# Two cross-attention stages of a fused Perceiver block on one core, unrolled and put into another order of a step

## The reference

```python
q, k, v = split_heads(x @ wq + bq), split_heads(ctx @ wk + bk), split_heads(ctx @ wv + bv)
attn = softmax(q @ k.T / sqrt(16) + neg)     # neg from the mask, xa0 only
attn = attn * group_prob                     # xa0 only
x = x + (attn @ v).reshape(B, S, 256) @ wo + bo
```

## Time and profile before

| | us |
|---|---|
| median of 3 runs | 1098.29 (1097.12 to 1099.25) |
| profiled execution, its own time | 1096.61 |
| its span, first to last instruction | 1094.7 |
| TensorE busy | 839.2 (77% of the span) |
| VectorE busy | 548.9 (50%) |
| ScalarE busy | 446.4 (41%) |
| GpSimd busy | 397.8 (36%) |
| xa0 on TensorE, from its first query projection to sa's first matmul | 187.5 |
| xa1 on TensorE, to ssm's first matmul | 195.9 |

### The profile page before, as it was taken

How to read it: one execution, slowest core, us unless ns; L and a number is a source line. 1 busy time by engine, 2 the same in 40 slices (tenths; PEclk the granted TensorE clock), 3 DMA queues, 4 the chain that set the end, 5 groups by cost and what they waited for, 6 DMA issues and landing times.

```text
span 1094.7 us, 21754 instructions
## 1 busy us (share of the span) xinstructions
PE 839.2 (77%) x6944; PEld 590.6 (54%) x6944; DVE 548.9 (50%) x1397; ACT 446.4 (41%) x1527; POOL 397.8 (36%) x577
## 2 busy tenths in 40 slices
PE   1899989689879658888987462677453999999990
PEld 0666666478754226666665341566341466666660
DVE  2477777568744343655655577576432222222222
ACT  1566666346614224656564102466400233333320
POOL 3356465535458754243344534222425000000005
PEclk9999999899969888999998765777655999999995
DMA  8121112633241634343233200211167034443004
GB/s 320 42 56 46 49 48 65 237 104 109 88 154 46 196 105 136 104 137 106 96 106 123 97 0 12 86 40 40 49 229 279 16 132 153 145 140 131 16 21 120
DMA packets 63723, 114.37 MB, mean 104 GB/s; under 512 B 6304, under 2 KB 20384, under 8 KB 62880
## 3 DMA queue, kind: packets, MB, share of 16 engines
q1 hardware_dynamic: 55488, 103.15, 28.0%
q10 hardware_dynamic: 6624, 6.03, 1.7%
q0 software_dynamic: 1536, 4.20, 1.3%
HBM read 79.02 MB, written 34.34 MB: 104 GB/s over the span
## 4 chain that ended last, share of the span: by engine, by line
PE 45%; ACT 15%; DVE 15%; POOL 10%; issue 9%; DMA 4%; SPq 1%; DVEq 0%; ACTq 0%; POOLq 0%
ACT probs L1116 6%; PE ps L967 4%; PE ps L969 4%; PE ps L968 4%; PE ps L524 3%; ACT probs L1075 3%; PE ps L567 3%; PE ps L583 2%; DMA ctx_t<-in_ctx 2%; DVE stat L1478 2%; PE ps L990 2%; PE ps L992 2%; PE ps L991 2%; ACT probs L1066 2%; PE ps L979 2%
## 5 line engine op out<-in xcount | busy, mean ns | idle before, releaser
L1266 POOL TENSOR_TENSOR var<-mv,half 128x1 f32<-128x1 f32 x56 | 11.0, 196 | 288.5 <-DVE mv L1479 201.2
L1298 POOL TENSOR_TENSOR piece_out<-piece_in,piece_out 128x512 f16<-128x512 f32 x96 | 112.7, 1173 | 7.7
L1966 DVE TENSOR_TENSOR probs<-ps,ctx_t 128x512 f32<-128x512 f32 x46 | 29.6, 686 | 155.0 <-PE ps L969 155.0
L567 PE MATMUL ps<-pack_const,probs 128*128 128x128 f32 x512 | 78.7, 291 | 28.8 <-DVE vbuf L1520 11.3
L1461 POOL DMA_INDIRECT pt<-y_rows,neg x16 | 15.4, 962 | 234.2 <-DMA y_rows<-vbuf 229.7
L1323 POOL TENSOR_TENSOR probs<-probs,gp 128x512 f32<-128x512 f32 x64 | 81.3, 1303 | 51.1 <-ACT probs L1066 51.1
L567 PEld LDWEIGHTS ps<-pack_const,probs 128*128 128x128 f32 x512 | 58.7, 146 | 53.2 <-DVE vbuf L1520 13.1
L1297 POOL CAST piece_out<-piece_in 128x512 f16<-128x512 f32 x96 | 62.2, 648 | 41.9 <-DMA piece_in<-in_w 40.7
L967 PE MATMUL ps<-arena,qbuf 128*128 x184 | 71.0, 386 | 0.0
L968 PE MATMUL ps<-arena,qbuf 128*128 x184 | 70.8, 385 | 0.0
L969 PE MATMUL ps<-arena,qbuf 128*128 x184 | 70.8, 385 | 0.0
(11 more groups left out here) (246 smaller groups left out, 2000.3 us busy)
## 6 DMA issues: line engine op xcount, KB each, us to landing
piece_in<-in_w SPq DMA_DIRECT2D x96, 256.0 KB, 2.8
w_parts<-piece_out SPq DMA_DIRECT2D x96, 256.0 KB, 2.0
arena<-w_parts SPq DMA_DIRECT2D x8, 3072.0 KB, 12.6
ctx_t<-in_ctx SPq DMA_DIRECT2D x32, 256.0 KB, 2.7
x_rows<-piece_out SPq DMA_DIRECT2D x1, 2944.0 KB, 16.7
qbuf<-x_rows ACTq DMA_DIRECT2D x23, 128.0 KB, 2.5
y_rows<-vbuf ACTq DMA_DIRECT2D x23, 128.0 KB, 1.7
arena<-in_xa SPq DMA_DIRECT2D x2, 1282.0 KB, 7.1
```

The source lines that it names most:

```text
L567: last = pe.transpose(AB[:, o:o + P], pr[:, 2 * c + n, kt * P:(kt + 1) * P], ident)
L1298: pool.tensor_tensor(both[:, PIECE:], src, both[:, 0:PIECE], ALU.subtract).then_inc(piece_split, 1)
```

## The change

All five engines run `step(k)` for k = 0 to 20 (`CROSS_STEPS` = `SEQS` + 5), each step with code of its own. Scores of a sequence are issued in one go, chunks 2 and 3 of a sequence move one step later, the mixed values to the end of a step, the steps that close a tile one step or more later. The context and the summed values have three buffers each; the third ones lie in unused columns of `qbuf`. The turned reciprocals move from AB[0:256] to M[256:512]. The diff, cut to its core and with the indentation reduced:

```diff
+spare = qbuf[:, :].bitcast(F32)
+contexts = [ctx_t[:, 0:DC * KEYS], ctx_t[:, DC * KEYS:2 * DC * KEYS], spare[:, 1024:1536]]
+values_of = [v32[:, 0:512], v32[:, 512:1024], spare[:, 1536:2048]]
+return 16 * (b // 3 + 1) + (16 * len(range(b % 3, SEQS, 3)) if st == "xa1" else 0)
+CROSS_STEPS = SEQS + 5
-    hold(sp, G[st]["v_projected"], b - 1)
+    hold(sp, G[st]["v_projected"], b - 2)
+    sp.dma_start(contexts[b % 3], src).then_inc(ctx_loaded[b % 3], 16)
...
-    def load_step(k, s, h):
-        if live(k, 0, SEQS):
-            load_context("xa0", k, s)
-        if live(k, 1, SEQS):
-            load_mask(k - 1, 1 - s)
-    skewed(sp, SEQS, 1, load_step)
+    for b in range(2, SEQS):
+        if b + 1 < SEQS:
+            load_context("xa0", b + 1)
+        load_mask(b, b % 2)
...
-    if k + 2 < SEQS:
-        load_context("xa1", k + 2, k % 2)
+    if 1 <= k < SEQS - 2:
+        load_context("xa1", k + 2)
...
-            hold(pe, g["r_copied"], b - 2)
+            hold(pe, g["pt_act"], 2 * b - 5)
-            hold(pe, g["pt_dve"], 2 * b - 2)
+            hold(pe, g["pt_dve"], 2 * b - 3)
+        hold(pe, g["xt"], h - 3)
+        hold(pe, g["resid"], h - 2)
...
             hold(pe, g["weighted"], 4 * b + c + 1)
             if c == 0:
-                hold(pe, g["k_copied"], at_most(b + 3, SEQS))
-                if isinstance(b, int) and b + 2 >= SEQS:
-                    hold(pe, g["r_copied"], b)
+                if b == 0:
+                    hold(pe, g["k_copied"], 3)
+                hold(pe, g["pt_act"], 2 * b)
             elif c == 1:
-                hold(pe, g["v_summed"], at_most(b + 2, SEQS))
-                if isinstance(b, int) and b + 1 >= SEQS:
-                    hold(pe, g["pt_dve"], 2 * b)
+                if b == 0:
+                    hold(pe, g["v_summed"], 2)
+                hold(pe, g["pt_dve"], 2 * b)
+            elif c == 2:
+                hold(pe, g["k_copied"], at_most(b + 4, SEQS))
+                hold(pe, g["pt_act"], 2 * b + 1)
             else:
-                hold(pe, g["pt_act" if c == 2 else "pt_dve"], 2 * b + 1)
+                hold(pe, g["v_summed"], at_most(b + 3, SEQS))
+                hold(pe, g["pt_dve"], 2 * b + 1)
...
         hold(pe, g["r_spread"], b + 1)
-        hold(pe, g["pt_act"], 2 * b + 2)
+        hold(pe, g["o_normed"], b)
         for f in range(2):
-            last = pe.transpose(AB[:, f * P:(f + 1) * P], spread[:, f * P:(f + 1) * P], ident)
+            last = pe.transpose(M[:, 256 + f * P:256 + (f + 1) * P], spread[:, f * P:(f + 1) * P], ident)
+        v = values_of[b % 3].rearrange("p (k n) -> p k n", k=2)
+        hold(pe, g["r_copied"], b + 1)
...
-    def step(k, s, h):
         if live(k, 0, SEQS):
-            if s == 0:
-                project_queries(h)
-            project_keys(k, s, h)
+            if k % 2 == 0:
+                project_queries(k // 2)
+            project_keys(k)
+        if live(k, 1, SEQS):
+            project_values(k - 1)
         if live(k, 3, SEQS):
-            mix_values(k - 3, 1 - s)
+            turn_reciprocals(k - 3)
+            turn_probs(k - 3, (k - 3) % 2, (2,))
+        if k % 2 == 1 and live(k, 5, SEQS):
+            join_heads((k - 5) // 2)
+        if k % 2 == 0 and live(k, 6, SEQS):
+            hold(pe, g["q_taken"], at_most(k // 2 + 1, TILES))
+            turn_rows(g, k // 2 - 3)
+        if live(k, 3, SEQS):
+            turn_probs(k - 3, (k - 3) % 2, (3,))
         if live(k, 1, SEQS):
-            project_values(k - 1, 1 - s)
-        for hf in range(2):
-            if live(k, 2, SEQS):
-                turn_probs(k - 2, s, (2 * hf, 2 * hf + 1))
-            if hf == 1 and live(k, 2, SEQS):
-                turn_reciprocals(k - 2)
-            if hf == 1 and live(k, 3, SEQS) and s == 0:
-                join_heads(h - 2)
-            if hf == 0 and live(k, 4, SEQS) and s == 1:
-                hold(pe, g["xt"], h - 2)
-                turn_rows(g, h - 2)
-            if live(k, 1, SEQS):
-                score(k - 1, 1 - s, h - 1 if s == 0 else h, hf)
-    skewed(pe, SEQS, 4, step)
+            for hf in range(2):
+                score(k - 1, (k - 1) % 2, (k - 1) // 2, hf)
+        if live(k, 2, SEQS):
+            turn_probs(k - 2, k % 2, (0, 1))
+        if live(k, 3, SEQS):
+            mix_values(k - 3, (k - 3) % 2)
+    for k in range(CROSS_STEPS):
+        step(k)
...
-        act.activation(turned_r[:, s * D:(s + 1) * D], AB[:, 0:D], ACT.Copy).then_inc(g["r_copied"].sem, 1)
+        act.activation(turned_r[:, s * D:(s + 1) * D], M[:, 256:512], ACT.Copy).then_inc(g["r_copied"].sem, 1)
+    def step(k):
+        pairs = range(PAIRS)
+        if live(k, 2, SEQS):
+            if st == "xa0":
+                exps(k - 2, k % 2, pairs)
+            else:
+                plain_exps(k - 2, k % 2, pairs[:4])
         if live(k, 0, SEQS):
-            copy_keys(k, s)
+            copy_keys(k, k % 2)
         if live(k, 2, SEQS) and st == "xa1":
-            plain_exps(k - 2, s)
-        for hf in range(2):
-            if live(k, 2, SEQS):
-                copy_probs(k - 2, s, 2 * hf)
-            if hf == 0 and live(k, 4, SEQS) and s == 1:
-                copy_turned(g, h - 2)
+            plain_exps(k - 2, k % 2, pairs[4:])
+        if live(k, 3, SEQS):
+            copy_reciprocals(k - 3, (k - 3) % 2)
+            copy_probs(k - 3, (k - 3) % 2, 2)
+        if k % 2 == 0 and live(k, 6, SEQS):
+            copy_turned(g, k // 2 - 3)
         if live(k, 2, SEQS):
-            copy_reciprocals(k - 2, s)
-        if live(k, 0, SEQS) and s == 0:
-            copy_queries(h)
-        if live(k, 1, SEQS) and st == "xa0":
-            exps(k - 1, 1 - s)
-    skewed(act, SEQS, 4, step)
+            copy_probs(k - 2, k % 2, 0)
+        if k % 2 == 0 and live(k, 0, SEQS):
+            copy_queries(k // 2)
+    for k in range(CROSS_STEPS):
+        step(k)
...
+    def step(k):
+        h = k // 2
+        if k % 2 == 0 and live(k, 0, SEQS):
             hold(pool, prev["normed"], h + 1)
             add_bias(g, h, w["bo"], prev["resid"] if st == "xa1" else prev["normed"])
+        if k % 2 == 0 and live(k, 6, SEQS):
+            root_of_variance(g, h - 3)
+        if live(k, 2, SEQS) and st == "xa0":
+            weigh(k - 2, k % 2)
         if live(k, 1, SEQS) and st == "xa0":
-            negate_mask(k - 1, 1 - s, h - 1 if s == 0 else h)
-        if live(k, 3, SEQS) and s == 0:
-            root_of_variance(g, h - 2)
-        if live(k, 1, SEQS) and st == "xa0":
-            weigh(k - 1, 1 - s)
-        if st == "xa1" and live(k, 3, SEQS) and s == 0:
-            hold(pool, g["normed"], h - 1)
+            negate_mask(k - 1, (k - 1) % 2, (k - 1) // 2)
+        if st == "xa1" and k % 2 == 0 and live(k, 6, SEQS):
+            hold(pool, g["normed"], h - 2)
             settle()
-            pool.tensor_copy(tile(xn_all, h - 2), xn[:, :]).then_inc(g["kept"].sem, 1)
-        if st == "xa1":
+            pool.tensor_copy(tile(xn_all, h - 3), xn[:, :]).then_inc(g["kept"].sem, 1)
+        if st == "xa1" and k < SEQS + 4:
             for j in range(2):
                 split_piece(j, k + XA1_PIECES // 2)
         chain.restart()
-    skewed(pool, SEQS, 4, step)
+    for k in range(CROSS_STEPS):
+        step(k)
...
-        hold(dve, g["pv_done"], b - 1)
+        hold(dve, g["pv_done"], b - 2)
-        on = scratch[:, 512:768]
-        chain.link(dve.tensor_tensor(on, M[:, 0:256], turned_r[:, s * D:(s + 1) * D], ALU.mult))
+        one, two_ = M[:, 256:384], scratch[:, 512:640]
+        chain.mark(dve.tensor_tensor(by_f(two_), sums[:, :, 1, :], shares[:, :, 1, :], ALU.mult))
+        chain.link(dve.tensor_tensor(by_f(one), sums[:, :, 0, :], shares[:, :, 0, :], ALU.mult))
-    def step(k, s, h):
-        closes = live(k, 3, SEQS) and s == 0
+    def step(k):
+        h = k // 2
+        if live(k, 2, SEQS):
+            (mask_scores if st == "xa0" else row_maxima)(k - 2, k % 2)
+        if live(k, 3, SEQS):
+            copy_probs(k - 3, (k - 3) % 2, 1)
+            spread_reciprocals(k - 3, (k - 3) % 2)
+        if live(k, 4, SEQS):
+            normalise_outputs(k - 4, k % 2, h - 2)
+        if k % 2 == 0 and live(k, 6, SEQS):
+            if st == "xa1":
+                hold(dve, g["kept"], h - 3)
+            hold(dve, g["turned"], h - 3)
+            normalise(g, h - 3, xn[:, :])
+        if k % 2 == 0 and live(k, 0, SEQS):
             take_queries(h)
+        if live(k, 1, SEQS):
+            sum_values(k - 1)
         if live(k, 3, SEQS):
-            normalise_outputs(k - 3, 1 - s, h - 2 if s == 0 else h - 1)
-        if live(k, 1, SEQS):
-            sum_values(k - 1, 1 - s)
-        if live(k, 2, SEQS):
-            copy_probs(k - 2, s, 1)
-            spread_reciprocals(k - 2, s)
-            copy_probs(k - 2, s, 3)
-        if closes:
-            add_output(g, h - 2, C[:, 256:512])
-            tile_stats(g, h - 2)
-        if live(k, 1, SEQS):
```

(58 more changed lines are left out.)

39 lines of the change are left out of this document (17 added, 22 removed).

## The result

The changed kernel takes 1059.82 us in the median (1056.85 to 1060.41, 4 runs) beside 1097.70 of the kernel before on the same chip: ratio 0.9646, interval 0.9619 to 0.9673. Its profiled execution took 1059.76 us with a span of 1057.9, so the span fell by 36.8 us. The forecast of 1065 and its range hold.

The account below looks back on a forecast made before the run. TensorE was taken as the bound, the rest as waits. Gains of 8.7 + 3.2 - 2 (xa0) and 20.8 + 4.1 - 2 (xa1), together 33 us, took 1096.61 to 1063.6; 1.7 more gave 1065, range 1050 to 1080 (own range 1054 to 1071).

Parts of the forecast that it names:

- (1): Both stages: issuing a sequence's scores in one burst instead of two halves saves 0.27 us a step, 0.5 a pair.
- (2): Both stages' regular parts: a pair of steps without any wait takes 18.8 us in xa0 and 19.0 in xa1.
- (3): xa0's six pairs: new waits of 1.1 and 0.35 us make a pair 20.2 us, gaining 1.45 each, 8.7 in all.
- (4): xa1's six pairs: no wait left, a pair takes 19.0 us, gaining 3.5 each, 20.8 in all.
- (5): Stage ends: first parts 23.9 and 26.5 us, tails 29.9 and 30.0; net gain taken as 3.2 and 4.1.
- the clock's share: Tails of both stages: 2 us a stage taken off the gain for matmuls at half speed.
- (6): Tails of both stages: gaps between matmul bursts send the clock back to 1.2 GHz, costing 2 us a stage.
- ACT keeping xa0 where it is: Rival, chance 0.18: small latencies between engines keep xa0's pairs at 21.7 us, only xa1 gains; 1074 us.
- POOL or transfers binding xa1: Rival, chance 0.10: POOL's pieces, stretched by transfer contention, make xa1's pairs 20.5 to 21.5 us; 12 us lost, 1077.
- Waits changing places: Rival, chance 0.03: TensorE's reciprocals wait for DVE's normalising and take back the gain; 1096 to 1100 us.
- Slower through code: Rival, chance 0.05: some 20 more steps of code, each fetch exposed for 2.7 us, add 54 us; 1119 us.

## Why the prediction held, step by step

The sum was right to 3.8 us of 33, out of terms that were off by more and in opposite directions, so that it came this close is in part luck.

**(1) The burst**: 0.27 us a step forecast. Between the same marks score groups cover 17.1 us of twelve steps before and 13.75 after in either stage, 0.28. Right in size. That it also shortens the step is shown for xa1; splitting the scores again made xa0's pairs 0.7 us longer.

**(2) A pair without waits** was mis-sized: 18.8 and 19.0 forecast, 18.0 measured in xa1 (107.9 / 6). TensorE's busy time fell by 12.0 us there (119.1 to 107.1), where I took off 6. The score groups give 3.4. The other groups' own sums fell by some 4: values from 24.0 to 22.8, since they took 2.00 us behind the mixing and take 1.90 behind the keys; joining from 6.8 to 6.2 and reciprocals from 5.5 to 4.6, of which the run with the loop written out has 6.2 and 4.9 already. The remaining 4 to 5 us are overlap of groups, which I had priced at 0.07 us a wait.

**(3) xa0**: 20.2 a pair forecast, 115.7 / 6 = 19.3 measured. The mechanism is as forecast, in place and in which steps: chunk 2 for the key copy in odd steps, 0.84 for 1.1, and chunk 3 for the value sum in even ones, 0.20 for 0.35. Idle time is 6.3 / 6 = 1.05 a pair for 1.45, and the rest is the gap-free pair, 18.2 for 18.8. That this wait is the price of xa0 was too simple: taken away, the same time stood at DVE, and at POOL after that. One term of DVE had the wrong sign. I added 0.15 us a step for a third operation of the normalising. Its sum of the two heads' parts before, in xa0's pairs:

```profile
L1574 DVE TENSOR_TENSOR ot<-scratch 128x128 f32<-128x128 f32 x12 | 13.8, 1153 | 0.4
```

With the operation ahead of it (421 ns) the normalising took 1.57 us a step; the three of now take 278, 283 and 292 ns, 0.85 us. That the change thus makes this step 0.7 us shorter on DVE, the forecast did not have. The spreading of the reciprocals, priced at no change, rose from 425 to 805 ns.

**(4) xa1**: no wait left, as forecast; the pair 18.0 for 19.0, by step (2). The contexts wait no more, but my step named the third buffer among the causes, and both runs on it say that it is none.

**(5) The first parts** failed: 23.9 and 26.5 forecast, 28.1 in both measured. (The net of xa0's ends has a slip besides: 6.5 - 2.9 is 3.6, not 3.4.) TensorE in xa0's, and DVE in step 3:

```profile
29.53 3.62 PE L531 MATMUL ps<-ctx_t,arena 128*128 128x256 f32 x8
...
49.95 2.94 PE L543 MATMUL ps<-arena,qbuf 128*128 128x256 f32 x8 [1.96 <-DVE pt L1552]
```

```profile
46.44 0.42 DVE L1577 CUSTOM_DVE_ANT_0 probs<-ps,neg 128x256 f32<-128x256 f32 x1 [2.05 <-POOL neg L1337]
```

The values of sequence 2 wait 1.96 us for DVE's copy of chunk 1, which in step 3 stands behind eight masks, and these wait 2.05 us for the negated mask, which stands behind POOL's first weighing; I had followed that copy in the regular steps only. The negation's place is what counts. In the run that negates first the copy still stands behind the masks, and the values wait 0.38 us; with that run's other edit alone, the key copy's, they wait 2.39. The row of the run that negates first:

```profile
48.35 1.99 PE L543 MATMUL ps<-arena,qbuf 128*128 128x256 f32 x8 [0.38 <-DVE pt L1552]
```

Of the 4.2 us missed, 2.3 belong to one execution. The run with the pieces last has the same code up to there and the same wait (1.95 us), and its first part took 25.8 us: its first keys took 2.48 us for 3.62, and its granted clock was 1.00 for 0.94. In xa1's first part the scores of sequence 1 wait for the exponentials of sequence 0, a wait that my step does not name, and behind it the granted clock was 0.69 (419.5 to 425.0):

```profile
419.57 2.09 PE L595 MATMUL ps<-kbuf,qbuf 32*128 32x256 f32 x16 [2.54 <-ACT probs L1091]
```

The tails: 33.0 and 32.9 us for 31.9 and 32.0 with the clock's share. POOL's last root stands behind four pieces, as forecast, and one piece waits 2.96 us for its load besides.

**(6) The clock**: 0.90 and 0.93 in the tails, higher than the 0.87 and 0.79 of before, though TensorE was busy a smaller share of them (60 and 53% for 64 and 64%), so this term can't be read off as a loss. It filled in for waits of the tails' chains, such as these of xa0:

```profile
175.87 2.58 PE L543 MATMUL ps<-arena,ctx_t 128*128 128x256 f32 x8 [2.35 <-DVE pt L1552]
...
187.86 0.66 PE L604 MATMUL ps<-pack_const,scratch 128*128 128x128 f32 x2 [3.90 <-DVE ot L1602]
```

In all, the pairs gave 40.6 us for 29.5, and the four ends with the clock's share -2.7 for 3.3: 11 us over, 6 under.

**The rivals.** ACT keeping xa0 where it is fell: 19.3 a pair, not 21.7. POOL or transfers binding xa1 fell: 0.8 us idle in six pairs. Waits changing places fell for the change as made, though xa0's experiments show just that mechanism for the next one. Slower through code fell: instruction fetches rose (below), and written-out code alone measured 1.0015.

## What to carry over

Order a pipelined step so that between a group and the next one that needs its copy out of the bank stands work of at least the copy's queue and length; one group moved wrongly (mixing, or chunk 2) cost more than the whole change gained. Count more than its length for a wait that goes, since groups that follow without a gap also overlap: 8.6 us of busy time went in xa1's pairs with 14.1 us of waits, the burst's 3.4 set apart (1.3 of the 8.6 went with the written-out loop, which made nothing shorter). Where the chains of several engines end a step close together, as in xa0 (115.7, 115.5 and 118.3 us), removing the wait that is named need not pay; follow each engine's queue to what it waits for, and take the start and end of the pipeline step by step, not as an average.
